# Router logits computed token-major, and batch 0 to 2's expert choice placed ahead of batch 3's first norm, in a one-core decoder layer

## The reference

```python
x = x + _layernorm(attn(_layernorm(x)))
x = x + _layernorm(ffn(_layernorm(x)))
# in ffn, T = 2048 tokens, d = 256, E = 8, K = 2, C = 640:
logits = jnp.einsum('td,de->te', x_flat, router)
topk_logits, sel = jax.lax.top_k(logits, K)
cw = jax.nn.softmax(topk_logits, axis=-1)
pos_all = jnp.cumsum(oh, axis=0) - oh          # place in the expert's queue, in order of tokens
valid = pos < C
buf = zeros((E, C, d)).at[e_flat, safe_pos].set(x_flat[tok], mode='drop')
h = silu(gate) * up; out_buf = h @ w_down
y = zeros((T, d)).at[tok].add(w[:, None] * gathered)
return y + shared_mlp(x_flat)
```

## Time and profile before

| | us |
|---|---|
| median of 3 runs | 794.25 (793.41 to 795.4) |
| profiled execution | 794.79 |
| its span, first to last instruction | 792.9 |
| PE busy | 745.7 (94%) |
| DVE busy | 593.1 (75%) |
| ACT busy | 496.7 (63%) |
| POOL busy | 562.5 (71%) |
| mean granted TensorE clock | 0.989 of 2.4 GHz |

### The profile page before, as it was taken

One profiled execution on the slowest core, in us unless ns is written; L12 is line 12 of the kernel. 1 busy time (PEld: TensorE's weight loads), 2 busy tenths in 40 slices (PEclk: granted clock), 3 DMA queues, 4 the chain that ended last, 5 costly groups with the idle time before them and its releaser, 6 DMA issues.

```text
span 792.9 us, 13984 instructions
## 1 busy us (share of the span) xinstructions
PE 745.7 (94%) x4340; PEld 626.4 (79%) x4340; DVE 593.1 (75%) x1548; ACT 496.7 (63%) x1165; POOL 562.5 (71%) x469
## 2 busy tenths in 40 slices
PE   5899999999999999999999999999899979999994
PEld 4677787888888888888888888888678878898762
DVE  6648787787988977888887788888582247775477
ACT  5778776777776767676676767676533245653352
POOL 4777898888888887888887888885137734341773
PEclk9999999999999999999999999999999989999998
DMA  9311155431212122221222222221142235541342
GB/s 310 122 43 54 54 167 172 135 108 57 72 63 70 66 70 64 68 68 68 68 68 67 68 68 68 68 67 42 47 123 98 99 115 198 197 145 72 96 124 95
DMA packets 47733, 75.74 MB, mean 96 GB/s; under 512 B 9712, under 2 KB 24624, under 8 KB 47664
## 3 DMA queue, kind: packets, MB, share of 16 engines
q1 hardware_dynamic: 43504, 65.19, 25.6%
q0 software_dynamic: 3072, 8.39, 3.3%
q10 hardware_dynamic: 1088, 1.31, 0.5%
HBM read 57.71 MB, written 17.17 MB: 94 GB/s over the span
## 4 chain that ended last, share of the span: by engine, by line
PE 75%; DVE 7%; POOL 5%; ACT 5%; issue 4%; DMA 2%; DVEq 0%; ACTq 0%; POOLq 0%
PE ps L387 22%; PE ps L911 16%; PE ps L876 14%; PE ps L927 10%; PE ps L897 8%; PE ps L1040 4%; POOL o_lo L1658 1%; POOL kh_row L1653 1%; POOL q_lo L1648 1%; POOL q_sw L1644 1%; POOL q_sw L1636 1%; DVE hid_both L1532 1%; ACT prob L598 1%; DVE hid_hi L1522 1%; DVE hid L1527 1%
## 5 line engine op out<-in xcount | busy, mean ns | idle before, releaser
L598 ACT ACTIVATE prob<-ps,neg_max 128x512 f32<-128x512 f32 (+3 forms) x256 | 132.7, 527 | 74.5 <-DVE neg_max L1224 74.5
L911 PE MATMUL ps<-pt,vp 128*128 128x512 f32 (+3 forms) x512 | 149.0, 433 | 2.0 <-DVE pt L1237 1.6
L911 PEld LDWEIGHTS ps<-pt,vp 128*128 128x128 f32 x512 | 82.6, 190 | 50.5 <-DVE pt L1237 16.8
L1224 DVE CUSTOM_DVE_ANT_0 ps<-ps,causal_row 128x512 f32<-128x512 f32 (+3 forms) x256 | 117.3, 519 | 0.1
L1658 POOL TENSOR_TENSOR o_lo<-o_t,o_hi 128x512 fp32r<-128x512 f32 x64 | 85.8, 1340 | 42.3 <-ACT o_hi L626 42.2
L1648 POOL TENSOR_TENSOR q_lo<-q_sw,q_hi 128x512 fp32r<-128x512 f32 x62 | 83.5, 1346 | 41.7 <-ACT q_hi L620 41.7
L897 PE MATMUL ps<-id_f,prob 128*128 128x128 f32 x640 | 92.3, 275 | 3.9 <-ACT pt L607 3.9
L1237 DVE TENSOR_SCALAR pt<-ps,vcol 128x384 f32<-128x384 f32 (+2 forms) x192 | 82.6, 476 | 7.7 <-PE ps L897 7.7
L876 PE MATMUL ps<-k_hi,q_hi 128*128 128x512 f32 x248 | 87.0, 351 | 0.0
L1644 POOL TENSOR_TENSOR q_sw<-q_cos,q_sw 128x512 f32<-128x512 f32 x62 | 78.8, 1271 | 8.9
L1636 POOL TENSOR_TENSOR q_sw<-q_sw,rope_sb 128x512 f32<-128x512 f32 x64 | 82.0, 1282 | 3.2 <-ACT q_sw L587 3.0
(11 more groups left out here) (214 smaller groups left out, 1919.3 us busy)
## 6 DMA issues: line engine op xcount, KB each, us to landing
kh_row<-kvh_rows SPq DMA_DIRECT2D x64, 256.0 KB, 3.1
inv_row<-inverse_sums SPq DMA_DIRECT2D x64, 256.0 KB, 3.1
slot_inputs<-zeros SPq DMA_DIRECT2D x8, 640.0 KB, 4.9
xg<-slot_inputs SPq DMA_DIRECT2D x8, 640.0 KB, 4.9
slot_outputs<-yo SPq DMA_DIRECT2D x8, 640.0 KB, 3.3
up_raw<-in_w_up_dram SPq DMA_DIRECT2D x8, 368.0 KB, 4.9
wo_raw<-in_wout_dram SPq DMA_DIRECT2D x4, 512.0 KB, 7.8
dn_sb<-in_w_dn_dram SPq DMA_DIRECT2D x8, 256.0 KB, 3.6
```

The lines of the kernel that those rows point to most:

```text
L598: ins = act.activation(prob[:, i % 2, ROW_AT[nt]:ROW_AT[nt] + w], ps_s[bank][:, at:at + w], ACT.Exp, scale=-1.0, bias=neg_max[:, i % 2, nt ...
L911: ins = pe.matmul(ps_qo[:, mt * P:SEQ], vp[:, b * TPB + mt, :], pt[:, i % 2, cols], start=(mt == 0), stop=(mt == PT_BANKS[-1][-1]))
L1224: ins = dve.tensor_tensor_reduce(s_, s_, causal_row[:, (NT - 1 - nt) * P:], 1.0, BIG, ALU.add, ALU.min, neg_max[:, i % 2, nt:nt + 1])
```

## The change

1. The logits are token-major. `xt_hi` and `xt_lo` of a 128-token tile are the stationary side, and the router moves: `rt_hl` holds its rounded columns and their low parts side by side, 16 columns. Per tile and half there are two products: xt_hi by 16 columns, which gives hi by hi and hi by lo in neighbouring columns, and xt_lo by the 8 rounded columns. ScalarE's copies and the transposes go. DVE adds the two groups of 8 columns.
2. Group 0's logits lie in bank 5, where `positions(0)` also writes. `shared_up` tile 2 needs that bank, so it now comes behind `pos_taken`, which DVE raises in `find_slots(0)`.
3. On DVE, `choose(0)`, one hidden product and `find_slots(0)` stand ahead of batch 3's `take_back`; two hidden products stand between its variance and its normalisation.
4. On POOL, `inverse_std2(3, 0)` moves from before the scatters to behind the third, and `inverse_std2(3, 1)` from behind the fourth to behind the eighth.
5. Batch 3's logits are computed behind `shared_up(2, [0])`.

```diff
@@ names and sizes
-        logit_rows = place("logit_rows", ROPE, [SEQ])
-        rt_hi, rt_lo = (small(n, [EO, 32], F32R) for n in ("rt_hi", "rt_lo"))
+        rt_hl = small("rt_hl", [EO, 2 * NE], F32R)
-        LOGIT_BANKS = [(4, 5, 3), (6,)]
-        TOKEN_BANK = [6, 7]
+        TOKEN_BANK = [5, 7]
@@ ScalarE
-            logits_copied(0)
             silus(0)
             silus(1)
             x_normed(B - 1)
             first_sum(0)
             turned_head(B - 1)
             first_sum(1)
-            logits_copied(1)
@@ TensorE
             def logits(g):
-                for n, b in enumerate(GROUPS[g]):
-                    pe.wait_ge(xt2_lo, (b + 1) * EO)
-                    ins = three_pass(pe, ps[LOGIT_BANKS[g][n]][0:32, :], lambda o: rt_hi[:, o, :],
-                                     lambda o: rt_lo[:, o, :], lambda o: xt_hi[:, o, tok(b)], lambda o: xt_lo[:, o, tok(b)])
-                ins.then_inc(logit_psum, 1)
-            def turn_logits(g):
-                pe.wait_ge(logit_copied, g + 1)
-                n = 32 * len(GROUPS[g])
-                for t in range(TPB):
-                    ins = pe.transpose(ps[TOKEN_BANK[g]][:, t * n:(t + 1) * n], logit_rows[0:n, t * P:(t + 1) * P],
-                                       id_f[0:n, 0:n])
+                ts = group_tiles(g)
+                for t in range(ts.start, ts.stop):
+                    pe.wait_ge(xt2_lo, (t // TPB + 1) * EO)
+                    at = (t - ts.start) * 2 * NE
+                    tokens = slice(t * P, (t + 1) * P)
+                    for o in range(EO):
+                        pe.matmul(ps[TOKEN_BANK[g]][:, at:at + 2 * NE], xt_hi[:, o, tokens], rt_hl[:, o, :],
+                                  start=(o == 0), stop=False)
+                        ins = pe.matmul(ps[TOKEN_BANK[g]][:, at:at + NE], xt_lo[:, o, tokens], rt_hl[:, o, 0:NE],
+                                        start=False, stop=(o == EO - 1))
                 ins.then_inc(token_psum, 1)
@@ TensorE, order
+            logits(0)
             pe.wait_ge(sw_split, 1)
-            logits(0)
-            shared_up(0, [0])
-            pe.wait_ge(y_taken, 2 * B)
-            turn_logits(0)
-            shared_up(0, range(1, SH))
+            shared_up(0, [0, 1])
             positions(0)
+            pe.wait_ge(pos_taken, 1)
+            shared_up(0, range(2, SH))
             shared_up(1)
             pe.wait_ge(sdn_in, 16 * len(RUNS))
-            pe.wait_ge(pos_taken, 1)
+            pe.wait_ge(y_taken, 2 * B)
             pe.wait_ge(s_hid_ready, SH + 1)
             shared_down(0)
             turn(B - 1)
             shared_down(1)
-            pe.wait_ge(sy_taken, 3)
-            logits(1)
+            pe.wait_ge(xt2_lo, B * EO)
             shared_up(2, [0])
             pe.wait_ge(sy_taken, 4)
-            turn_logits(1)
+            logits(1)
@@ VectorE, choose
-                turned = ps[TOKEN_BANK[g]][:, 0:TPB * n * 32].rearrange("p (t b c) -> p t b c", t=TPB, b=n)
-                done(dve.tensor_copy(logit[:, ts, :].rearrange("p (b t) e -> p t b e", b=n), turned[:, :, :, 0:NE]))
+                parts = ps[TOKEN_BANK[g]][:, 0:(ts.stop - ts.start) * 2 * NE].rearrange("p (t c) -> p t c", c=2 * NE)
+                done(dve.tensor_copy(logit[:, ts, :], parts[:, :, NE:]))
+                done(dve.tensor_tensor(logit[:, ts, :], parts[:, :, 0:NE], logit[:, ts, :], ALU.add))
@@ VectorE, order
             rest_of_turned(2)
+            choose(0)
+            shared_hidden(0, [0])
+            find_slots(0)
             take_back(B - 1)
             stats_of_y(B - 1)
             variances(B - 1)
+            shared_hidden(0, range(1, SH))
             for t in range(TPB):
                 normalize_y(B - 1, t)
-            choose(0)
-            shared_hidden(0, [0, 1])
-            find_slots(0)
-            shared_hidden(0, range(2, SH))
@@ GpSimd
-                pool.tensor_copy(rt_hi[:], rt_raw[:]).then_inc(rt_hi_ready, 1)
+                pool.tensor_copy(rt_hl[:, :, 0:NE], rt_raw[:, :, 0:NE]).then_inc(rt_hi_ready, 1)
-                pool.tensor_tensor(rt_lo[:], rt_raw[:], rt_hi[:].bitcast(F32), ALU.subtract)
+                pool.tensor_tensor(rt_hl[:, :, NE:], rt_raw[:, :, 0:NE], rt_hl[:, :, 0:NE].bitcast(F32), ALU.subtract)
-            inverse_std2(B - 1, 0)
             pool.wait_ge(slots_cleared, 8 * 16)
             for g in range(len(GROUPS)):
                 ts = group_tiles(g)
                 pool.wait_ge(slots_ready, g + 1)
                 for t in range(ts.start, ts.stop):
-                    if t == 2:
+                    if t == 4:
                         inverse_std2(B - 1, 1)
                     for k in range(2):
+                        if t == 1 and k == 1:
+                            inverse_std2(B - 1, 0)
                         pool.indirect_dma_start(
```

More of the change, by code:

```diff
@@ L295, in decoder_layer @@
             sem("s_psum_g"), sem("s_silu"), sem("s_hid_ready"), sem("sy_psum"), sem("sy_taken"))
-        logit_psum, logit_copied, token_psum = (
-            sem("logit_psum"), sem("logit_copied"), sem("token_psum"))
+        token_psum = sem("token_psum")
         gap_ready, egap_ready, rows_known = sem("gap_ready"), sem("egap_ready"), sem("rows_known")
@@ L646, in silus @@
                     act.activation(s_sg[0:w, i, :], ps[2 * i][0:w, :], ACT.Silu).then_inc(s_silu, 1)
[L648 to L652, removed]
             def factors_as_columns(k):
@@ L1402, in choose @@
                 ts = group_tiles(g)
-                n = len(GROUPS[g])
                 dve.wait_ge(token_psum, g + 1)
-                turned = ps[TOKEN_BANK[g]][:, 0:TPB * n * 32].rearrange("p (t b c) -> p t b c", t=TPB, b=n)
-                done(dve.tensor_copy(logit[:, ts, :].rearrange("p (b t) e -> p t b e", b=n), turned[:, :, :, 0:NE]))
+                parts = ps[TOKEN_BANK[g]][:, 0:(ts.stop - ts.start) * 2 * NE].rearrange("p (t c) -> p t c", c=2 * NE)
+                done(dve.tensor_copy(logit[:, ts, :], parts[:, :, NE:]))
+                done(dve.tensor_tensor(logit[:, ts, :], parts[:, :, 0:NE], logit[:, ts, :], ALU.add))
                 for t in range(ts.start, ts.stop):
```

## The result

| | before | after |
|---|---|---|
| median, runs on the same chip | 794.78 us (793.41 to 798.27, 17 runs) | 797.7 us (794.72 to 800.53, 17 runs) |
| ratio after to before | | 1.0032, 95% interval 1.0021 to 1.0043 |
| profiled execution, its span | 794.79, 792.9 | 797.24, 795.4 |
| mean granted clock | 0.989 | 0.986 |

The kernel became slower by 2.5 us by the ratio and 2.9 by the medians, where no change was forecast. The forecast was 794.6 for the profiled execution and 794.0 for the median; they took 797.24 and 797.7, above the range of 791.0 to 796.8. Over all 17 runs of the kernel after, the mean granted clock has a median of 0.984 (0.981 to 0.988), so the profiled execution doesn't overstate what the clock lost.

The account below looks back on a forecast made before the run. Two chains ending within 3.4 us of each other, POOL's scatters and PE's own work, were taken to bound the passage between attention and experts. Sum +0.45 + 1.7 - 2.3 = -0.15: 794.6 profiled, 794.0 median; range 791.0 to 796.8.

Parts of the forecast that it names:

- 48 x 0.111 = 5.33: Logits on PE: 48 narrow products at the value products' pitch take 5.33 us, ending at 577.7, 1.1 later than before.
- The forecast's own sign: Logits on PE: the forecast is wrong if they take under 4 or over 7 us.
- The rival of dear loads: Logits on PE: weight loads show in full, 0.19 a product, PE 3.8 us later, 797.8; chance 0.10.
- Cheap products: Logits on PE: at 0.05 a product 789.7 or 791.4, at 0.08 everything 1.45 earlier; chance 0.10.
- Choice: `choose(0)` on DVE: starts at 577.85 and takes 4.99 us to the next product, where it took 4.70.
- the rest of the chain: From DVE's choice onward: positions' copy at 583.5, first scatter at 586.6, PE's turn of the slots at 637.65.
- The two new stalls: PE waits 0.7 us at `pos_taken` and 2.4 before `shared_down(0)`, for the hidden product.
- The fall behind that stall: After PE's 2.4 us stall the clock falls once; half of 3.4 us of work is lost, +1.7.
- Expert 0: Expert 0 on PE: without 3.37 us of idleness ahead it takes about 10.5 instead of 12.86, -2.3.
- The wait of POOL for `at_in`: Scatters on POOL: batch 3's `at_in` comes at 621.4, and POOL waits 0.7 to 1 us for it.
- The balance: PE's turn of the slots at 637.65, 0.45 us later than before; whole sum +0.45 + 1.7 - 2.3 = -0.15.
- the stall happens but the clock holds: Rival for PE's stall before `shared_down(0)`: no clock fall follows, +0.45 - 2.3 = -1.85, 792.4; chance 0.22.

Follow-up runs that it names:

- the wide kernel: Against the kernel after: the router's 16 columns pass eight times per product, 128 moving columns with the same weight loads; 792.38 us, ratio 0.9968.
- the old order: Against the kernel after: narrow logits kept, DVE's and POOL's order put back as before; 796.82 us, ratio 1.0026.

## Why the prediction was wrong

- **The step that failed** is the term "48 x 0.111 = 5.33" in the form in which the sum used it: that PE keeps its full clock while it does these products and the two tiles behind them. The pitch of 0.111 was right, for 24 of them. The clock's falls were looked for only behind idle stretches, and none was weighed for a stretch in which the engine is busy throughout. What the runs showed in its place: the clock fell after 24 of them, the logits took 7.91 us (5.39 in the wide kernel) and the first shared tile 5.11 (2.76 in the sum), 4.84 us in all that the sum put at nothing. With the same 48 loads and 128 columns the clock holds and the time is 5.1 to 5.3 us less. The forecast's own sign fired: it was to be wrong if the logits took over 7 us.
- The rival of dear loads had about the right time (797.8) with the wrong mechanism. Its condition, a pitch of about 0.16, is even met on average (7.91 / 48 = 0.165), but as 0.112 and then 0.213, and not because loads show in full: the wide kernel has the same loads at 0.112. That it came near is luck. Cheap products, at 0.05 or 0.08, are out as well: 0.112 at 8, 16 and 128 columns. The load is what these have in common, so it most likely sets the pitch; a load of another size wasn't tried. "TensorE: Matmul & The Clock Gate" of the Trainium skill, section "Back-to-back issue gap", has 81 ns for 128 columns; here the pitch of such pairs is 112, and the measurement decides. "TensorEngine Tiling (Array Packing)" of the Trainium skill, section "When to Use Tiling", swaps sides where the moving one has at most 64 columns, together with column tiling. The time agrees in sign (ratio 1.0032), but through the clock.
- **Choice**: 5.2 on DVE (580.77 to 585.97), 5.00 in the wide kernel (577.60 to 582.60), 4.99 forecast. With a held clock, in the wide kernel, the rest of the chain came out too: positions at 582.92 (583.2), first scatter at 586.28 (586.6), turn of the slots at 637.06 (637.65). In the kernel after all of it is later: positions 588.43, first scatter 591.79, turn 642.57.
- **The two new stalls** are where they were forecast: 0.48 at `pos_taken` (0.7), and 1.70 ahead of `shared_down(0)` for the hidden product (2.4). The second was too large because the first scatter took 1.23 and not the 2.12 of the earlier trace rows.
- **The fall behind that stall** (+1.7) didn't come: the clock is 1.00 from 590 to 655, with 1.70 as with 1.68 in the wide kernel. The forecast chose it since 2.4 was nearer to 2.70 than to 1.59; at 1.7 that argument goes the other way.
- **Expert 0** took 10.65 (645.45 to 656.10), 10.5 forecast: the gain of 2.2 is real. The wait of POOL for `at_in` was 1.49, forecast 0.7 to 1.
- **The balance**: the turn of the slots is 5.38 later than before (642.57 against 637.19). 0.32 was there before the logits (572.68 against 572.36), 4.84 is the half clock, and 0.22 is what the wide kernel needs more than the one before from there on (65.05 against 64.83), where 0.45 was forecast. Expert 0 gives back 2.2, and at expert 1's start the kernel is 3.16 late (656.10 against 652.94). Its span is 2.5 longer: 0.7 is regained behind that point, in a part which the change doesn't touch.
- The rival "the stall happens but the clock holds", 792.4, is what the wide kernel does: 792.38, with a stall of 1.68 and the clock at 1.00. It was right for another kernel than the one that was made, and with a smaller stall than its own 2.4, so that the two times agree to 0.02 is luck.

What stays open: what about few moving columns lets the clock fall (columns in the array, results written, or the share of time spent on loads), since the experiment changes all three together. Every kernel here, narrow or wide, also has an idle of about 1.27 us on PE and eight transposes just ahead of the logits (571.84 in the kernel after). In the wide ones the clock holds behind it, so it isn't enough by itself; whether 48 narrow products let the clock fall without it wasn't tried. Nor were widths between 16 and 128, or roots on another engine than POOL. Why the half clock lasts for 10.3 us, well into products of 512 columns, isn't shown either.

## What to carry to other kernels

When a rewrite trades few wide products for many with hardly any moving columns, sum their pitch from the trace, but also ask what the clock will do under them: here PE was busy all the time and ran at half clock. Where the pitch stays the same with more columns, as here up to 128, repeating the moving side costs nothing, and it can hold the clock for what comes behind. And an early result is worth only what the engine that needs it can take: look for the neighbour that becomes late as the first wait goes.

## What the runs showed of the hardware

- Under products of 16 and 8 moving columns, 0.112 apart and behind an idle of 1.27, the clock fell to 1.2 GHz after 2.6 us in the kernel after and 3.0 us with the old order (571.35 to 574.40). Under the 16 of batch 3, 616.50 to 618.1, with no idle ahead, it stayed at 1.00. In the wide kernel it stayed at 1.00 as well.
- At half clock the same products are 0.213 apart, with 128 columns at full clock 0.112: the pitch of a load and a short product followed the clock, not the columns.
- Idle stretches of PE (two numbers: two stretches close together) and what followed: 1.70 or 1.68 alone, no fall; 1.46 and 1.21 with little between, about 3.4 us of half clock (0.66 over 5 us); 2.09 and 0.61, about 6.8 us; 0.73 and 1.60, no fall (1.00 over 640 to 655); 3.37 and 1.60 in the kernel before, about 6.9 us.
